# State-space layer: input products of every second state on TensorE, tiled state sums, twelve states read out by GpSimd

## Chip, cores and metric

The kernel runs on one core of a Trainium2 chip. The metric is the device time of one execution in microseconds (us); lower is better. A core has TensorE (PE, matrix products into PSUM), VectorE (DVE), ScalarE (ACT) and GpSimd (POOL), each with an in-order queue of its own, and SyncE (SP), which here only issues DMAs.

## What is computed

A language-model tower over 64 sequences of 128 tokens with 192 features: embedding and layer norm, attention, a layer of four experts, a bidirectional state-space layer, a layer of eight experts (two per token). The change touches the state-space layer alone. Of the reference, cut to what matters:

```python
def _mamba(x, W_in, conv_w, conv_b, W_xproj, W_dt, b_dt, A_log, D_param, W_out):
    xp, z = jnp.split(x @ W_in.T, 2, axis=-1)                  # 384 inner channels each
    xc = silu(causal_depthwise_conv(xp, conv_w, 4 taps) + conv_b)
    dt, Bt, Ct = jnp.split(xc @ W_xproj.T, [12, 12 + 16], axis=-1)
    dt = softplus(dt @ W_dt.T + b_dt)
    A = -jnp.exp(A_log)                                        # 384 x 16
    def step(h, inp):                                          # scan over the 128 tokens
        dt_t, B_t, C_t, x_t = inp
        dA = jnp.exp(dt_t[..., None] * A)
        h = dA * h + (dt_t * x_t)[..., None] * B_t[:, None, :]
        y = jnp.einsum('bdn,bn->bd', h, C_t)
        return (h, y)
    ...
    y = (y + xc * D_param) * silu(z)
    return y @ W_out.T
return 0.5 * (_mamba(x) + _mamba(x reversed in time) reversed)
```

## The kernel before, in words

The phases follow each other; the state-space phase (`mamba_phase`) takes the 64 sequences in 16 groups of four (512 tokens in the free dimension) and each group in two directions. The 384 channels are DC = 3 blocks (c) of 128 partitions, the NS = 16 states (n) are done one by one, so a half (one group, one direction) has 48 units p = 3n + c. In each unit

- ScalarE (`act_decay`) writes dA = exp(dt * A) for one block into one of four PSUM banks (`RING`, banks 3 to 6); where the bank held something else, it also zeroes the edge column of each sequence.
- GpSimd (`pool_dBx`, line 1804) writes the input products u * B_n of all three blocks at once into one of eight SBUF slots `xh`. B_n, the same for every partition, has been loaded by DMA (`sp_B_in`) from DRAM, where `sp_BC_out` stored it, broadcast over partitions.
- VectorE (`dve_scan`, line 1773) runs the recurrence h = dA * h + product over 512 columns.
- The read-out h * C_n is done by VectorE block by block (`dve_read`, line 1784) or, for the states in `BY_POOL` (8 in one direction, 6 in the other), by GpSimd in one instruction of three blocks (`pool_read`, line 1793).
- TensorE (`pe_sum`, line 1731) adds the read-outs of all states into banks 0 to 2 by matmuls with the identity, one per block and state; `pe_D` adds xc * D in the same way with a diagonal. A sum lags its scan by LAG = 3 states.

Beside these units run the steps of the next half, placed by hand at units given by the table `POS`: row additions and layer norm, transposes (`pe_zT`), input projection (`pe_x`, `pe_gate`), convolution by diagonal matrices (`pe_conv`, line 1579), projection to dt, B, C, softplus in three identity matmuls (`pe_sp`, line 1666, over u, lw and r; r is completed by a DMA that accumulates, issued by GpSimd in `pool_add`), u = dt * xc (`dve_u`, line 1675). TensorE's results of these steps pass through the one bank NB = 7, and each is copied out before the next. At the end of a group `dve_y` gates the sums and `pe_out` (line 1743) projects them. Each engine's queue follows the order of `slot`: in the units of a half, its own work (`main`) and the steps placed there.

Matmuls are in fp32; each shows as two weight loads and two matmul records in the trace, a transpose as one. The attention phase, which the change leaves as it is, has matmuls on 16 rows at four 32-row offsets (line 552, one after another for r = 0 to 3, each r to a bank of its own) and matmuls with 32 output columns at four 32-partition offsets of one bank (line 575), 12 matmuls each.

Of the kernel before, what the change touches and what calls it, by code (L numbers as in the profile page):

```python
# [15 lines left out]
P = 128  # L16
# [1306 lines left out]
PB, PD, PJ = 64, 96, 44  # L1323

# [30 lines left out]
def mamba_phase(nc, A, H, bank, K, Y, BCd, W):  # L1355
# [5 lines left out]
    with Phase(nc) as ctx:  # L1361
# [3 lines left out]
        NQ, QN = 8, 2  # L1365
        UNITS = NS * DC
        POS = {
            "y": (6, 7, 9), "pe_D0": (14, 15, 17), "pe_D1": (6, 16, 25), "pe_out": (17, 18), "out": (14, 15),
            "act_rows": (11, 13), "rows": (12, 14), "stats": 14, "rstd": 18, "norm": 40,
# [3 lines left out]
            "act_pj": (15, 10), "act_xc": (14, 8), "act_e": (23, 23), "act_w1": (23, 26), "act_ln": (26, 29),  # L1373
            "pe_sp0": (26, 36, 40), "act_sp0": (30, 39, 41), "u0": (34, 38, 41), "pe_sp1": (32, 38, 42), "act_sp1": (34, 38, 40),
            "u1": (32, 37, 40),
        }
        NB = 7
        BY_POOL = (0, 3, 4, 5, 10, 12, 13, 14), (0, 6, 9, 10, 11, 14)
        RING = ((3, 4, 5, 6) * 2 + (3, 4, 5, 3, 4, 5, 3) + (6, 4, 5, 3) * 8 + (6,),
                (4, 5, 3, 6, 4, 3, 5, 6) + (3, 4, 5, 6) * 10)  # L1380
        ROWS_BANK, ROWS_FROM, ROWS_TO = 6, 7, 15

        def before_in_bank(d, p):

            b, back = RING[d][p], 0
            while True:
                p -= 1
                if p < 0:
                    p, d, back = UNITS - 1, 1 - d, back + 1
                if RING[d][p] == b:  # L1390
                    return back, d, p
# [10 lines left out]
        dg, dgD = sb("dg", [P, DC, TAPS, P]), sb("dgD", [P, DC, P])  # L1402
# [4 lines left out]
        z = sb("z", [P, G, C])  # L1407
# [6 lines left out]
        lw = sb("lw", [P, DC, TOK])  # L1414
        gz = sb("gz", [P, DC, TOK])
# [27 lines left out]
        with nc.Block() as block:  # L1443
            @block.vector
            def _(dve):
# [3 lines left out]
                for c in range(DC):  # L1449
                    for k in range(TAPS):  # L1450
                        dve.tensor_scalar(dg[:, c, k, :], K.ident[:, :], cw[:, c, k:k + 1], None, ALU.mult)
# [610 lines left out]
```

## Time and profile before

| | |
|---|---|
| median of 3 runs | 4727.18 us (4723.77 to 4732.5) |
| profiled execution, first to last instruction | 4718.1 us |
| median less that span | 9.1 us |
| state-space phase in it | some 1145 to 3822 us |
| busy in the whole span: PE, DVE, ACT, POOL | 4271.6, 3251.1, 2430.7, 3212.3 us |

The profiled execution is one execution of the program; busy times, durations and waits below are its own. A group of instructions stands with its line, engine, operation, what it writes <- reads, its shape and its count. Matmuls are pipelined and their ends are modelled, so the distance from one start to the next tells more of TensorE's pace than the length of one.

### The profile page before, as it was taken

How to read it: one execution, taken by the hardware profiler on the slowest of the kernel's cores; microseconds unless marked ns; L12 is line 12 of the kernel's file. 1: busy time of each engine (PE TensorE's matmuls, PEld its weight loads, DVE VectorE, ACT ScalarE, POOL GpSimd, SP SyncE). 2: the span in 40 equal slices, each digit the busy share in tenths (PEclk: the TensorE clock that was granted, in tenths of full speed). 3: DMA queues.
4: the chain of work that ended last, by engine and by line, in shares of the span. 5: the costliest groups of instructions: out<-in, count | busy, mean ns of one | idle time of the engine just before them, and what ended most of it. 6: DMA issues, size and time to landing. Idle time of an engine off the chain costs nothing. (4 is left out here: it accounts for less than half of the span.)

```text
span 4718.1 us, 62490 instructions
## 1 busy us (share of the span) xinstructions
PE 4271.6 (91%) x16896; PEld 2235.4 (47%) x16896; DVE 3251.1 (69%) x5016; ACT 2430.7 (52%) x4880; POOL 3212.3 (68%) x1669
## 2 busy tenths in 40 slices
PE   7999986997899999999999999999999876999994
PEld 4666644664343443344334434433443334666673
DVE  5667773111699999999999999989999975111114
ACT  3555542122566666767676666667666633222221
POOL 3222222442799999999999999999999941444441
PEclk9999996998899999999999999999999987999997
DMA  1000011342334333334333333333333321333456
GB/s 35 21 20 20 20 53 59 108 127 76 107 114 125 115 118 116 121 109 121 122 112 115 112 121 118 116 118 113 117 107 123 114 67 45 110 116 112 127 169 219
DMA packets 267113, 478.79 MB, mean 101 GB/s; under 512 B 39404, under 2 KB 176444, under 8 KB 266908
## 3 DMA queue, kind: packets, MB, share of 16 engines
q1 hardware_dynamic: 235776, 403.02, 26.9%
q0 software_dynamic: 28032, 73.17, 6.1%
q14 instruction: 171, 1.40, 0.1%
q10 hardware_dynamic: 3100, 0.64, 0.1%
q8 instruction: 34, 0.56, 0.1%
HBM read 409.75 MB, written 41.81 MB: 96 GB/s over the span
## 5 line engine op out<-in xcount | busy, mean ns | idle before, releaser
L1804 POOL TENSOR_TENSOR m_xh<-m_u,m_Bb 128x1536 f32<-128x1536 f32 x512 | 1780.1, 3550 | 51.6 <-DVE m_u L1675 39.0
L1731 PE MATMUL bank<-m_xh,ident 128*128 128x512 f32 x3072 | 1455.1, 609 | 34.3 <-POOL m_xh L1793 34.3
L1773 DVE TENSOR_TENSOR_SCAN bank<-bank,m_xh 128x512 f32<-128x512 f32 x864 | 1038.9, 1216 | 44.5 <-ACT bank L1760 42.2
L1760 ACT ACTIVATE bank<-m_dt,m_Ac 128x508 f32<-128x508 f32 x1536 | 1024.9, 683 | 38.4 <-DVE m_xh L1773 38.4
L1731 PEld LDWEIGHTS bank<-m_xh,ident 128*128 128x128 f32 x3072 | 576.2, 194 | 820.0 <-issue 730.7
L1773 DVE TENSOR_TENSOR_SCAN m_xh<-bank,m_xh 128x512 f32<-128x512 f32 x672 | 787.8, 1207 | 64.8 <-ACT bank L1760 59.3
L1793 POOL TENSOR_TENSOR m_xh<-m_xh,m_Cb 128x1536 f32<-128x1536 f32 x224 | 794.0, 3544 | 4.3 <-DVE m_xh L1773 4.0
L1784 DVE TENSOR_TENSOR m_xh<-bank,m_Cb 128x512 f32<-128x512 f32 x864 | 581.3, 673 | 10.9 <-DMA m_Cb<-BC_rows 10.8
L1204 ACT ACTIVATE f1t_h<-bank,f1t_b 128x512 f32<-128x512 f32 (+1 forms) x276 | 147.6, 586 | 509.9 <-PE bank L1234 509.9
L1134 POOL DMA_INDIRECT rows_y<-f1t_y,f1t_home x142 | 139.9, 985 | 316.4 <-DVE f1t_y L1175 287.1
L1579 PE MATMUL bank<-m_xp,m_dg 128*128 128x512 f32 x768 | 351.9, 601 | 3.7 <-DVE m_u L1675 1.4
L1243 PE MATMUL bank<-f1t_w,f1t_h 128*128 128x192 f32 x1704 | 289.0, 329 | 19.4 <-ACT f1t_h L1204 19.4
L1243 PEld LDWEIGHTS bank<-f1t_w,f1t_h 128*128 128x128 f32 x1704 | 275.7, 190 | 31.6 <-issue 28.1
L1759 ACT COPY bank<-m_none 128x4 f32<-128x4 f32 x896 | 144.2, 161 | 260.5 <-DVE m_xh L1784 171.3
L1164 DVE COPY f1t_xTa<-bank 128x512 f32<-128x512 f32 (+1 forms) x46 | 26.2, 570 | 342.2 <-PE bank L1215 342.2
L97 POOL TENSOR_SCALAR ln_e_ve<-ln_e_mv 128x4 f32<-128x4 f32 x16 | 3.7, 229 | 348.2 <-DVE ln_e_mv L91 348.2
L1579 PEld LDWEIGHTS bank<-m_xp,m_dg 128*128 128x128 f32 x768 | 142.9, 190 | 201.6 <-issue 157.0
L373 DVE TENSOR_REDUCE mx<-bank 128x3 f32<-128x384 f32 x256 | 141.0, 551 | 113.4 <-PE bank L552 112.1
L1231 PE MATMUL bank<-f1t_xTa,f1t_w1a 128*128 128x512 f32 (+1 forms) x552 | 217.1, 516 | 1.6 <-DVE f1t_xTb L1167 1.6
L1175 DVE TENSOR_TENSOR f1t_y<-bank,f1t_b 128x192 f32<-128x192 f32 x142 | 50.8, 358 | 216.7 <-PE bank L1243 216.7
L1204 ACT ACTIVATE f0t_h<-bank,f0t_b 128x512 f32<-128x512 f32 (+1 forms) x132 | 71.9, 596 | 246.5 <-PE bank L1234 246.5
L454 ACT COPY ST<-bank 128x384 f32<-128x384 f32 x256 | 120.8, 472 | 143.0 <-PE bank L562 143.0
(367 smaller groups left out, 6148.3 us busy)
## 6 DMA issues: line engine op xcount, KB each, us to landing
m_Bb<-BC_rows SPq DMA_DIRECT2D x256, 512.0 KB, 4.8
m_Cb<-BC_rows SPq DMA_DIRECT2D x256, 512.0 KB, 4.0
f1t_w<-f_w SPq DMA_DIRECT2D x46, 576.0 KB
m_r<-m_dt POOLq DMA_DIRECT2D x32, 768.0 KB, 7.4
f1t_w1a<-f_w SPq DMA_DIRECT2D x46, 384.0 KB
f0t_w<-f_w SPq DMA_DIRECT2D x22, 576.0 KB
f1c_yg<-rows_y SPq DMA_DIRECT2D x16, 768.0 KB, 8.3
f1t_w1b<-f_w SPq DMA_DIRECT2D x92, 96.0 KB
```

What stands on the lines that cost most here:

```text
L373: dve.reduce_max(mx[:, u % NE, :], s_ps, AX).then_inc(s_mx, 1)
L1204: act.activation(h[b][:, m, 0:w * P], bank[:, HB[(s2 + m) % 4], 0:w * P], ACT.Gelu, bias=b1[b][:, m:m + 1]).then_inc(s_gelu, 1)
L1231: pe.matmul(o[f], w1a[b][:, (m + f) * P:(m + f + 1) * P], xTa[b][:, 0:w * P], start=True, stop=False)
L1243: mm = pe.matmul(bank[:, YB[j % 2], 0:C], h[b][:, m, j * P:(j + 1) * P], w2[b][:, m, :], start=(m == 0), stop=(m == HK - 1))
L1579: mm = pe.matmul(bank[:, front(c), :], dg[:, c, k, :], xp[:, c, :, o:o + P], start=(k == 0), stop=(k == TAPS - 1))
L1731: mm = pe.matmul(bank[:, c, :], K.ident[:, :], xh[n % NX][:, c, :], start=False, stop=(d == 1 and n == NS - 1))
L1759: act.copy(o[:, :, edge:edge + 1], none[:, :].unsqueeze(2))
L1760: act.activation(o[:, :, lo:hi], seqs(dt[d][:, c, :])[:, :, lo:hi], ACT.Exp, scale=Ac[:, c, n:n + 1]).then_inc(s_dA, 1)
L1773: dve.tensor_tensor_scan(o, bank[:, RING[d][p], way], xh[n % NX][:, c, way], 0.0, ALU.mult, ALU.add).then_inc(s_h, 1)
L1784: dve.tensor_tensor(xh[n % NX][:, c, :], bank[:, RING[d][p], :], Cb[q % RC][:, n % QN, :], ALU.mult).then_inc(s_prv, 1)
L1793: pool.tensor_tensor(v, v, Cb[q % RC][:, n % QN, :].unsqueeze(1).to_broadcast([P, DC, TOK]), ALU.mult).then_inc(s_prp, 1)
L1804: pool.tensor_tensor(xh[n % NX][:, :, :], u[d][:, :, :], Bb[q % RB][:, n % QN, :].unsqueeze(1).to_broadcast([P, DC, TOK]), ALU.mult).then_ ...
```

## The change

- `BY_PE`: for the eight odd states the input products come from TensorE. u is transposed per sequence (`pe_uT`, copied to `uT` by `act_uT`), B of these states too (`pe_BT`, `act_BT`). ScalarE writes, per state and sequence, B on the diagonal of a 128x128 matrix (`act_Bd`), and `pe_fill` multiplies: uT (stationary) by that diagonal, four matmuls of 128 columns per unit, into a PSUM ring bank, EARLY = 3 units ahead of the scan. The decay of these states goes to SBUF (`dA`, three buffers).
- GpSimd makes the products of the eight even states, and reads out twelve states in both directions (all but 2, 6, 10, 14).
- `pe_sum` and `pe_D` do the three blocks of a state in one step of 12 matmuls on 32x32 tiles (`turned`): block c's rows of strip q go to output strip (q + c) mod 4, so that the 12 tiles lie on different places of the array; weights for z and the output are permuted on the way in. `pe_conv` becomes four diagonal 32x32 tiles per tap.
- Rows are added to H by one accumulating DMA per group, issued by GpSimd (`pool_rows`), instead of load, two copies and two additions.
- B is loaded one state at a time into two buffers (before: two states, four buffers). The ring is plain p mod 4. Positions in `POS` change.

```diff
+QUADS, QP = 4, 32
+BY_PE = (1, 3, 5, 7, 9, 11, 13, 15)
+BY_GP = tuple(n for n in range(16) if n not in BY_PE)
...
-        BY_POOL = (0, 3, 4, 5, 10, 12, 13, 14), (0, 6, 9, 10, 11, 14)
+        BY_POOL = tuple(n for n in range(NS) if n not in (2, 6, 10, 14)), tuple(n for n in range(NS) if n not in (2, 6, 10, 14))
+        RINGS = 4
+        ring = lambda p: 3 + p % RINGS
...
-        RB, RC = 4, 2
+        RB, RC = 2, 2
...
-        NX, AHEAD, LAG = 8, 2, 3
+        NX, AHEAD, LAG, EARLY = 8, 2, 3, 3
+        NDA, NBD = 3, 2
...
+            def pool_rows(pool):
+                rows = Y[0:B * P, :].rearrange("(t p) c -> p t c", p=P)
+                pool.dma_start(H[:, bass.ds(gl * G, G), :], rows[:, bass.ds(gl * G, G), :], accum_op=ALU.add).then_inc(s_added, 16)
...
                 for k in range(TAPS):
                     o = k if d == 0 else 2 * (TAPS - 1) - k
-                    mm = pe.matmul(bank[:, front(c), :], dg[:, c, k, :], xp[:, c, :, o:o + P], start=(k == 0), stop=(k == TAPS - 1))
+                    for q in range(QUADS):
+                        i = slice(q * QP, (q + 1) * QP)
+                        mm = pe.matmul(bank[i, front(c), :], dg[i, c, k, :], xp[i, c, :, o:o + P], start=(k == 0), stop=(k == TAPS - 1))
...
+            def pe_uT(pe, c):
+                pe.wait_ge(s_u, s * DC + c + 1)
+                stand_alone(pe, K.go)
+                for b in range(G):
+                    mm = pe.transpose(bank[:, front(c), b * P:(b + 1) * P], u[d][:, c, b * P:(b + 1) * P], K.ident[:, :])
+                mm.then_inc(s_uTps, 1)
...
+        def turned(c):
+            for q in range(QUADS):
+                o = (q + c) % QUADS
+                yield slice(q * QP, (q + 1) * QP), slice(o * QP, (o + 1) * QP)
...
-        def pe_sum(pe, g, d, n, c):
+        def pe_sum(pe, g, d, n):
             if n not in BY_POOL[d]:
-                pe.wait_ge(s_prv, dve_reads(g, d, n) + c + 1)
-            elif c == 0:
+                pe.wait_ge(s_prv, dve_reads(g, d, n) + DC)
+            else:
                 pe.wait_ge(s_prp, pool_reads(g, d, n + 1))
-            mm = pe.matmul(bank[:, c, :], K.ident[:, :], xh[n % NX][:, c, :], start=False, stop=(d == 1 and n == NS - 1))
+            stand_alone(pe, K.go)
+            for c in range(DC):
+                for i, o in turned(c):
+                    mm = pe.matmul(bank[o, c, :], K.ident[i, i], xh[n % NX][i, c, :], start=False, stop=(d == 1 and n == NS - 1))
             mm.then_inc(s_red, 1)
...
+        def pe_fill(pe, g, d, p):
+            n, c = divmod(p, DC)
+            s = g * 2 + d
+            k = by_pe(n)
+            if c == 0:
+                pe.wait_ge(s_Bd, (s * NPE + k + 1) * G)
+            if k == 0:
+                pe.wait_ge(s_uT, s * DC + c + 1)
+            bank_free(pe, g, d, p)
+            stand_alone(pe, K.go)
+            for b in range(G):
+                t = slice(b * P, (b + 1) * P)
+                mm = pe.matmul(bank[:, ring(p), t], uT[d][:, c, t], Bd[k % NBD][:, b, :], start=True, stop=True)
+            mm.then_inc(s_fill, 1)
+
+        def act_Bd(act, g, d, n, b):
...
+            act.activation(Bd[k % NBD][:, b, :], K.ident[:, :], ACT.Identity, bias=none[:, 0:1], scale=BT[d][:, b, k:k + 1]).then_inc(s_Bd, 1)
...
+            if n in BY_PE:
+                dve.wait_ge(s_fill, fills(g, d, fill_no(p) + 1))
+                decay, add = dA[fill_no(p) % NDA][:, way], bank[:, ring(p), way]
+                if c == 0:
+                    slot_free(dve, g, d, n)
             else:
-                o = bank[:, RING[d][p], way]
-            dve.tensor_tensor_scan(o, bank[:, RING[d][p], way], xh[n % NX][:, c, way], 0.0, ALU.mult, ALU.add).then_inc(s_h, 1)
+                if c == 0:
+                    dve.wait_ge(s_dBx, s * NGP + by_gp(n) + 1)
+                decay, add = bank[:, ring(p), way], xh[n % NX][:, c, way]
+            o = xh[n % NX][:, c, way] if n in BY_POOL[d] else bank[:, ring(p), way]
+            dve.tensor_tensor_scan(o, decay, add, 0.0, ALU.mult, ALU.add).then_inc(s_h, 1)
```

## Rows read from the trace of the kernel before

**Rows 1.** The page: span, busy time, and two engines over 40 slices (tenths).

```profile
span 4718.1 us, 62490 instructions
PE 4271.6 (91%) x16896; PEld 2235.4 (47%) x16896; DVE 3251.1 (69%) x5016; ACT 2430.7 (52%) x4880; POOL 3212.3 (68%) x1669
...
PE   7999986997899999999999999999999876999994
...
DVE  5667773111699999999999999989999975111114
...
POOL 3222222442799999999999999999999941444441
```

**Rows 2.** Line 1828, the store of B and C, once a half.

```profile
L1828 SPq DMA_DIRECT2D BC_rows<-m_low x32: 348/360/427, 1182.6 to 3701.2; - x32
```

**Rows 3.** Windows: one whole group; length, busy (records) by engine, clock, DMA.

```profile
core 0: us, PE busy (x) PEld busy (x) DVE busy (x) ACT busy (x) POOL busy (x), PEclk, DMA share, GB/s
...
2393.00:2555.50 162.50, 156.44 (x367) 65.12 (x367) 148.56 (x171) 108.04 (x208) 159.34 (x53) 0.99 0.38 115
```

**Rows 4.** Timeline of GpSimd; start, length.

```profile
2326.17 3.65 POOL L1793 TENSOR_TENSOR m_xh<-m_xh,m_Cb 128x1536 f32<-128x1536 f32 x1
2329.56 3.65 POOL L1804 TENSOR_TENSOR m_xh<-m_u,m_Bb 128x1536 f32<-128x1536 f32 x1
2332.96 3.63 POOL L1793 TENSOR_TENSOR m_xh<-m_xh,m_Cb 128x1536 f32<-128x1536 f32 x1
```

**Rows 5.** Groups by line and shape, same group; busy, mean ns | idle before.

```profile
L1731 PE MATMUL bank<-m_xh,ident 128*128 128x512 f32 x192 | 90.0, 604 | 0.0
...
L1579 PE MATMUL bank<-m_xp,m_dg 128*128 128x512 f32 x48 | 21.9, 598 | 0.1
...
L1743 PE MATMUL bank<-m_wo,m_r 128*128 128x192 f32 x24 | 4.2, 326 | 0.0
```

**Rows 6.** Timeline of TensorE: state sums without a gap.

```profile
2304.62 7.89 PE L1731 MATMUL bank<-m_xh,ident 128*128 128x512 f32 x18
```

**Rows 7.** Timeline of VectorE.

```profile
2311.12 1.22 DVE L1773 TENSOR_TENSOR_SCAN bank<-bank,m_xh 128x512 f32<-128x512 f32 x1
2312.25 0.67 DVE L1784 TENSOR_TENSOR m_xh<-bank,m_Cb 128x512 f32<-128x512 f32 x1
2312.84 1.22 DVE L1773 TENSOR_TENSOR_SCAN bank<-bank,m_xh 128x512 f32<-128x512 f32 x1
```

**Rows 8.** Waits from 2080 to 3700 us, 20 halves; total, times, longest.

```profile
ACT m_dt L1671 <- PE bank L1666: 169.6, 60, 5.0
...
PE bank L1666 <- DMA m_r<-m_dt: 43.7, 20, 3.8
```

**Rows 9.** The page's DMA issues: times, size, us to landing.

```profile
m_r<-m_dt POOLq DMA_DIRECT2D x32, 768.0 KB, 7.4
```

**Rows 10.** Timeline of TensorE in the attention phase.

```profile
418.90 0.95 PE L552 MATMUL bank<-qT 16*128 16x128 f32 x24
419.78 1.13 PE L528 MATMUL bank<-zTa,wqp_a 128*128 128x512 f32 x2
...
421.60 0.49 PE L562 MATMUL bank<-ident,S 128*128 128x128 f32 x3
422.02 0.86 PE L575 MATMUL bank<-ST,V 128*32 128x128 f32 x24
422.82 0.70 PE L528 MATMUL bank<-zTa,wqp_a 128*128 128x512 f32 x1
```

**Rows 11.** Windows inside line 575: records in flight, PE then PEld.

```profile
422.00:422.04 0.04, 0.02 (x3) 0.02 (x3) 1.00 0.00 0
422.04:422.08 0.04, 0.04 (x4) 0.04 (x8) 1.00 0.00 0
422.28:422.32 0.04, 0.04 (x12) 0.04 (x6) 1.00 0.00 0
```

**Rows 12.** Timeline of ScalarE.

```profile
2389.63 0.15 ACT L1759 COPY bank<-m_none 128x4 f32<-128x4 f32 x1
2389.72 0.69 ACT L1760 ACTIVATE bank<-m_dt,m_Ac 128x508 f32<-128x508 f32 x1
2390.34 0.58 ACT L1568 COPY m_gz<-bank 128x512 f32<-128x512 f32 x1
2390.82 0.17 ACT L1759 COPY bank<-m_none 128x4 f32<-128x4 f32 x1
...
1441.64 1.85 ACT L1516 ACTIVATE m_z<-H,m_mrs,m_ln_rs 128x192 f32 x4
```

More of the change, by code:

```diff
@@ L1392, in mamba_phase @@
+        NPE, NGP = len(BY_PE), len(BY_GP)
+        by_pe = lambda n: sum(k < n for k in BY_PE)
+        by_gp = lambda n: sum(k < n for k in BY_GP)
+        fill_no = lambda p: by_pe(p // DC) * DC + p % DC
+        fills = lambda g, d, k: ((g * 2 + d) * NPE * DC) + k
         of_pool = lambda d, n: sum(k < n for k in BY_POOL[d])
@@ L1514, in act_norm @@
                 act.wait_ge(s_mrs, gl * 2 + 2)
+                if not first:
+                    stand_alone(act, K.go)
+                    act.wait_ge(s_spps, (s + 1) * DC)
                 for j in range(G):
@@ L1641, in act_ln @@
                 act.wait_ge(s_w1, s + 1)
-                if not first:
+                act.wait_ge(s_zTps, g * 2 + 2)
+                if d == 1:
+                    stand_alone(act, K.go)
                     act.wait_ge(s_spps, s * DC)
@@ L1675, in dve_u, with act_uT @@
                 dve.tensor_tensor(u[d][:, c, :], bank[:, front(c), :], xc[d][:, c, :], ALU.mult).then_inc(s_u, 1)
+            def pe_uT(pe, c):
[4 more added lines that the diff above has]
+                mm.then_inc(s_uTps, 1)
+            def act_uT(act, c):
+                act.wait_ge(s_uTps, s * DC + c + 1)
+                if c == 0 and deep:
+                    act.wait_ge(s_fill, (s - 1) * NPE * DC)
+                act.copy(uT[d][:, c, :], bank[:, front(c), :]).then_inc(s_uT, 1)
             todo = {"pe": [], "act": [], "dve": [], "pool": []}
@@ L1682, in chain @@
                 at = (lambda p: p - 100) if first else (lambda p: p)
-                for i in two:
-                    put("act", at(POS["act_rows"][i]), act_rows, i)
-                    put("dve", at(POS["rows"][i]), dve_rows, i)
+                put("pool", at(POS["rows"]), pool_rows)
                 put("dve", at(POS["stats"]), dve_stats)
@@ L1749, in act_decay @@
             lo, hi, edge = (1, P, 0) if d == 0 else (0, P - 1, P - 1)
-            o = seqs(bank[:, RING[d][p], :])
-            back, db, pb = before_in_bank(d, p)
             if p == 0:
                 act.wait_ge(s_sp, (g * 2 + d + 1) * DC)
-            if d == 0 and p == ROWS_TO and not (isinstance(g, int) and g == NG - 1):
-                act.wait_ge(s_added, g * 2 + 4)
-            elif back == 0 or later(g, d):
-                released(act, g if db <= d and back < 2 else g - 1, db, pb)
@@ L1758, in act_decay @@
-            if back or pb // DC not in BY_POOL[d] or d == 0 and p == ROWS_TO:
+            if n in BY_PE:
+                f = fill_no(p)
+                o = seqs(dA[f % NDA][:, :])
+                if f >= NDA:
+                    act.wait_ge(s_h, (g * 2 + d) * UNITS + BY_PE[by_pe(n) - 1] * DC + c + 1)
+                elif later(g, d):
+                    act.wait_ge(s_h, (g * 2 + d - 1) * UNITS + BY_PE[-1] * DC + c + 1)
+                zero = f < NDA
+            else:
+                o = seqs(bank[:, ring(p), :])
+                back, db, pb = before_in_bank(d, p)
+                bank_free(act, g, d, p)
+                zero = back or pb // DC in BY_PE or pb // DC not in BY_POOL[d]
@@ L1930, in main @@
                     n, c = divmod(p, DC)
-                    if c == 0 and not (end and n >= NS - AHEAD):
+                    if c == 0 and (n + AHEAD) % NS in BY_GP and not (end and n >= NS - AHEAD):
                         pool_dBx(pool, *at_step(g, d, n + AHEAD))
@@ L2028, in layout @@
     import numpy as np
+    turned = np.concatenate([c * P + (q - c) % QUADS * QP + np.arange(QP) for c in range(DC) for q in range(QUADS)])
+    as_is = np.arange(DC * P)
     g = lambda n: np.asarray(inputs[n])
```

259 lines of the change are left out of this document (146 added, 113 removed), and 3 rows, old and new, of the table POS.

## The prediction

> **What bounds the kernel now.** I read the page first: over the span TensorE is busy most, but in the slices of the state-space phase GpSimd stands at nine tenths or more in almost every one, and TensorE and VectorE too [rows 1]. So three engines run near their limit there, and the question is which has no slack. The unit for that is one half (one direction of one group of four sequences: 16 states of 3 blocks). The store of B and C happens once a half; 32 of them from 1182.6 to 3701.2 us give 2518.6/31 = 81.2 us a half [rows 2]. Only what shortens that counts, 32 times.
>
> The windows of one whole group (two halves, 162.5 us) show GpSimd 159.3 busy, TensorE 156.4, VectorE 148.6, ScalarE 108.0 [rows 3]. Busy time of overlapping instructions misleads, so I take start-to-start distances where an engine runs without a gap.
> - GpSimd: a product or read-out of 128x1536 starts every 3.40 us [rows 4]. Before, a half has 16 products and 7 read-outs: 23 x 3.40 = 78.2 of 81.2. The other 3.0 are the start of the accumulating DMA, the norm's small operations and waits.
> - TensorE: each fp32 matmul leaves two records. The group has 368 expected and 367 shown [rows 3]: 192 for state sums, 48 for the convolution, 24 of 192 columns for the output [rows 5], 8 transposes, and 96 more of 512 columns by the code. 18 records of 512 columns take 7.89 us with an end of 0.6: 0.43 each [rows 6]. 336 x 0.43 + 24 x 0.17 + 8 x 0.11 = 149.5, so 74.7 a half, 92%.
> - VectorE: a scan costs 1.13 us and a read-out 0.59 [rows 7]: 48 x 1.13 + 27 x 0.59 (on average of the two directions) + some 4.5 for u, y, rows, output and statistics = 74.6.
> - ScalarE: 54 [rows 3].
>
> So GpSimd sets the pace with some 1 us of true idle time a half, and TensorE and VectorE follow 6 us behind. The chain of waits shows what else holds the in-order queues: ScalarE waits for TensorE's softplus sum (169.6 us in 20 halves), and TensorE for the DMA into m_r (43.7 in 20, 2.2 a half) [rows 8].
>
> **The change, engine by engine, a half.**
>
> GpSimd: 8 products instead of 16, 12 read-outs instead of 7: 20 x 3.40 = 68.0; of the 3.0 beside them some 1.6 stay of known work, and the rows' accumulating DMA adds 0.4. That is 70.0, or 71.2 with the same idle time.
>
> VectorE: 15 read-outs fewer, -8.8, and the two additions of rows go: about 65.5. Scans keep one PSUM and one SBUF operand; only which is which changes, so 1.13 stays.
>
> ScalarE: two row copies go, three copies of u's transpose come at 0.5 (a copy of 512 columns, start to start) [rows 12], and 32 activations of 128x128 that write B on a diagonal. Not in the trace; a copy of 4 columns takes 0.09 start to start and 192 columns with a scale column 0.44 [rows 12]. I take 0.30, between them: 9.6, bounds 3 and 14. ScalarE comes to 65, bounds 58 and 69. Fewer zeroed edges take some 1 off. That is hidden as long as TensorE or GpSimd needs more; with the 8.5 a half that it waits for L1666 today (169.6 / 20 [rows 8]) it would reach 73.5, so it has lost most of its cover.
>
> TensorE, where I expect the bound:
> - State sums. 48 matmuls of 128x128 (41.3 us) become 16 steps of 12 matmuls on 32x32 tiles, and D's three (2.6) one such step. If the tiles run at once a step costs two passes, 0.86. The attention stage shows half of that: 12 matmuls on four row strips (L552) and 12 on four column strips (L575) take 24 records of 128 columns in 0.95 and 0.86 us to the last end, 0.80 to 0.88 until the next step starts [rows 10]; one after another they would take 24 x 0.11 = 2.6. The windows inside L575 show three records started in 40 ns, four in flight, later twelve by the modelled ends [rows 11]. So four streams at once are seen over row strips and over column strips; twelve over both are not. Lower bound 0.86, upper bound 3 x 0.86 = 2.58 if the three blocks of a state follow each other. It is nearest to L575, whose streams share all rows as the three blocks here do, so I take 0.86 and 0.08 for staggered starts: 17 x 0.94 = 16.0.
> - Switches between full and tiled passes: L552 and L575 cost 0.88 and 0.80 against 6 waves of 0.11 = 0.66 [rows 10], so about 0.2 a step. 16 sums and 3 convolution blocks: 19 x 0.2 = 3.8.
> - Products of every second state: 24 units of 4 matmuls, 8 records of 128 columns. Bounds: a quarter of the 512-column record, 0.107, and the 192-column record, 0.17. Transposes of 128 columns with a weight load each start 0.11 to 0.12 apart (three of L562, 0.49 with an end of 0.27) [rows 10]; I take 0.115: 22.1, bounds 20.5 and 33.
> - 12 transposes of u, 12 x 0.11 = 1.3; the four small ones of B, 0.9.
> - Convolution: each 128x128 matmul becomes four diagonal tiles. At once, they cost the same 12 x 0.86 = 10.3; softplus 7.7, dt and projection 5.2, x or gate 5.2, output 2.0, row transposes 0.5 are unchanged.
> Sum: 16.0 + 3.8 + 22.1 + 2.2 + 30.9 = 75.0. TensorE then has more work than GpSimd's 70.0, so it takes over as the bound, at about its old load.
>
> TensorE's queue is in order, and a product unit is issued only three units before its scan (some 4 us). Its waits used to be covered by sums that lag three states. Now behind a TensorE wait (softplus for the DMA into m_r, 7.4 us from issue to landing [rows 9]) stand products that VectorE needs next. I add what TensorE waits now for that DMA, 2.2, rounded to 2.0: 77.0 a half. The loads of B shrink by half or more and keep one state of lead; the C loads keep two buffers, each freed by GpSimd's later read-outs, with some 3 units to spare; I cost both at nothing.
>
> Sum: (77.0 - 81.2) x 32 = -134. Once: transposing B and u before the first half +3. The profiled execution: 4718.1 - 131 = 4587; the median of the runs is 9.1 above that span, so 4596, and I say 4595.
>
> **A rule against it.** The attention stage's row strips (L552) write four different banks, its column strips (L575) one; four row strips into one bank, as the convolution and each block's sum do here, no row shows. "TensorEngine Tiling (Array Packing)", Gotcha 1, in the Trainium skill says that different row tiles cannot access the same PSUM bank simultaneously. Taken word for word this would serialise them (the fourth rival). I weigh it low, since each strip writes its own 32 partitions, as L575's do.
>
> **Rivals.**
> 1. GpSimd stays the bound (TensorE at its lower ends: products 20.5, switches near 0, sums 13.8, some 68). 71.2 a half, so -320 + 3: 4410. For: 0.107 is what the columns cost. Against: switch gaps are visible.
> 2. Coupling. Nothing overruns, but TensorE, in the loop of VectorE's scans, loses 2.5 to 7 us more a half in round trips over its one front bank (now also for u's transposes): 79.5 to 84, 4675 to 4820. For: ScalarE's long waits for L1666. Decides from 4.2 us a half.
> 3. The three blocks of a state pass one after another, sharing row strips: a step costs 2.66, +1.72 x 17 = +29 a half: 106, about 5520. This is the slower case by one mechanism; it decides as soon as a step costs above 1.2 us. For: in L552 the three column blocks of one strip do follow each other. Against: L575. Half of it (each block's second pass ahead of the next block, 1.72 a step) gives 5020. "TensorE: Matmul & The Clock Gate", part 3, in the Trainium skill says weight loads overlap running matmuls only where the row group differs, which would bring this rival about; it also reports sixteen tiles at once, which would not.
> 4. Row strips of one bank exclude each other: sums and D 17 x 9.4 more, convolution 31 more: some 270 a half, above 10,000 us.
>
> **How the numbers follow.** Forecast (74 to 79 a half, 4500 to 4660) 0.45; rival 1, 0.15; rival 2, 0.20; rival 3, 0.12, its half 0.05; rival 4, 0.02; 0.01 left. The range must leave out no more than 0.2: from 4420 (most of rival 1) to 4860 (all of rival 2). A measurement of this kernel can tell about 0.2%, 9 us, which is 0.3 us a half. Faster: 0.45 + 0.15 + 0.04 of rival 2 = 0.64. Same 0.04, the narrow part of rival 2 about 81.2 a half. Slower: the rest, 0.32.
>
> **What would show it.** Start to start, a state's sum of 24 records should take about 0.95 us and be followed within 0.2 by the next step; 8 records of a product unit 0.92; halves 77 apart by the store of B and C; in the windows TensorE without idle time, GpSimd at 90%, VectorE at 85, ScalarE at 85. Wrong would be: a sum over 1.2 us, GpSimd without gaps, or VectorE waiting for TensorE's products while TensorE stands at L1666 or u's transposes.

## The result and the profile after

The changed kernel takes 5416.3 us (5413.1 to 5416.7, four runs), the kernel before in the same comparison 4729.8 (4723.8 to 4733.7): ratio 1.1456, 95% interval 1.1438 to 1.1473. It is slower by 686 us; the forecast was 4595, range 4420 to 4860. The prediction was wrong, in sign too.

The page of the changed kernel, span, busy time and two engines over 40 slices, answers to [rows 1]:

```profile
span 5414.6 us, 102448 instructions
PE 4577.8 (85%) x35776; PEld 2682.9 (50%) x35776; DVE 2970.8 (55%) x4508; ACT 2853.3 (53%) x5840; POOL 2920.9 (54%) x1589
...
PE   7999879968888888888888888888888887799994
DVE  5777641116665666666566656666666676411114
...
POOL 2222124417676676667666766766766674244442
PEclk9999979979898898888888989888998988899997
```

GpSimd and VectorE, at nine tenths before, stand mostly at six or seven, and TensorE at eight. No engine is full, and yet the phase is longer. The store of B and C (now line 1917) gives the length of a half, as [rows 2] did:

```profile
L1917 SPq DMA_DIRECT2D BC_rows<-m_low x32: 318/326/430, 1184.9 to 4381.1; - x32
```

(4381.1 - 1184.9)/31 = 103.1 us a half, against 81.2. All of the loss is there: 21.9 x 32 = 701 us, against 697 between the two profiled executions.

Windows of the same stretch as [rows 3], and one of 400 us, by the same columns:

```profile
core 0: us, PE busy (x) PEld busy (x) DVE busy (x) ACT busy (x) POOL busy (x), PEclk, DMA share, GB/s
2400.00:2800.00 400.00, 340.10 (x2984) 179.18 (x2982) 255.17 (x270) 257.93 (x514) 269.77 (x90) 0.89 0.26 73
...
2393.00:2555.50 162.50, 135.76 (x1180) 73.62 (x1179) 107.77 (x117) 106.43 (x210) 111.18 (x39) 0.88 0.27 73
```

Times 103.1/400, a half holds 69.5 us of GpSimd's work, 66.5 of ScalarE's, 65.8 of VectorE's: the forecast had 70, 65 and 65.5. These three sums were right to 2 us, and each engine now stands idle for a third of the half. TensorE is 87.7 busy against 75 forecast, at a granted clock of 0.89 (0.99 in [rows 3]). Busy time counts more than starts do: before, the window had 78.2 a half where the prediction's sum gave 74.7. That leaves some 9 us that the forecast did not have.

Single operations cost what was forecast, too. TensorE's timeline (start, length; in brackets the idle time before and who ended it), where it runs without a gap:

```profile
2586.23 1.11 PE L1776 MATMUL bank<-m_xc,m_dgD 32*32 32x512 f32 x24
2587.27 1.16 PE L1815 MATMUL bank<-m_Bd,m_uT 128*128 128x128 f32 x8
2588.36 1.11 PE L1787 MATMUL bank<-m_xh,ident 32*32 32x512 f32 x24
...
2593.70 1.11 PE L1787 MATMUL bank<-m_xh,ident 32*32 32x512 f32 x24
2594.75 1.16 PE L1815 MATMUL bank<-m_Bd,m_uT 128*128 128x128 f32 x8
```

D's step of 24 records takes 1.04 us to the next start and a state's sum 1.05, product units 1.09 (forecast: 0.94 and 0.92, and 0.2 for each switch between full and tiled). The twelve tiles run at once: 24 records of 0.43 one after another would take 10.3. GpSimd's operations start 3.40 apart as before (2570.17 to 2573.57, shown below).

What fills the half are waits. The list of waits, 2080 to 3900 us, 17.7 halves (total, times, longest), against [rows 8]:

```profile
POOL m_xh L1888 <- DVE m_xh L1868: 321.2, 125, 7.1
...
DVE m_xh L1868 <- ACT m_dA L1847: 177.1, 61, 7.7
ACT m_xc L1602 <- PE bank L1594: 171.4, 51, 10.2
...
POOL m_xh L1899 <- PE bank L1787: 152.6, 33, 7.6
ACT m_dt L1654 <- PE bank L1644: 152.3, 45, 6.7
DVE m_xh L1868 <- PE bank L1815: 150.4, 47, 6.2
DVE m_xh L1868 <- ACT bank L1847: 124.5, 47, 4.8
```

Read it as a circle. GpSimd's read-outs (L1888) wait for scans, scans (L1868) for ScalarE's decays (L1847) and for products (L1815), ScalarE at the convolution (L1602) and at dt (L1654) for TensorE, and GpSimd's products (L1899) for TensorE's sums. Most waits are short (the first line is 2.6 each), and each engine is late because of another. One place shows how; first TensorE:

```profile
2570.60 3.62 PE L1594 MATMUL bank<-m_xp,m_dg 32*32 32x512 f32 x32
2575.27 3.65 PE L1594 MATMUL bank<-m_xp,m_dg 32*32 32x512 f32 x32 [1.04 <-ACT m_xc L1602]
2579.81 3.22 PE L1594 MATMUL bank<-m_xp,m_dg 32*32 32x512 f32 x28 [0.89 <-ACT m_xc L1602]
2582.44 0.80 PE L1787 MATMUL bank<-m_xh,ident 32*32 32x512 f32 x8
...
2584.25 2.05 PE L1815 MATMUL bank<-m_Bd,m_uT 128*128 128x128 f32 x16
```

then ScalarE,

```profile
2574.44 0.69 ACT L1602 ACTIVATE m_xc<-bank,m_cb 128x512 f32<-128x512 f32 x1 [3.83 <-PE bank L1594]
...
2578.98 0.69 ACT L1602 ACTIVATE m_xc<-bank,m_cb 128x512 f32<-128x512 f32 x1 [1.68 <-PE bank L1594]
```

VectorE,

```profile
2575.83 1.23 DVE L1868 TENSOR_TENSOR_SCAN bank<-bank,m_xh 128x512 f32<-128x512 f32 x1 [3.33 <-ACT bank L1847]
...
2585.53 1.22 DVE L1868 TENSOR_TENSOR_SCAN m_xh<-m_dA,bank 128x512 f32<-128x512 f32 x1 [6.17 <-PE bank L1815]
```

and GpSimd:

```profile
2570.17 3.44 POOL L1899 TENSOR_TENSOR m_xh<-m_u,m_Bb 128x1536 f32<-128x1536 f32 x1 [1.31 <-DMA m_Bb<-BC_rows]
2573.57 3.43 POOL L1888 TENSOR_TENSOR m_xh<-m_xh,m_Cb 128x1536 f32<-128x1536 f32 x1
2584.55 3.46 POOL L1899 TENSOR_TENSOR m_xh<-m_u,m_Bb 128x1536 f32<-128x1536 f32 x1 [7.55 <-PE bank L1787]
```

The next half's convolution stands at positions 3, 4 and 5 of TensorE's in-order queue. Its three blocks share one front bank, so each waits for ScalarE's copy of the one before: they start 4.6 us apart, 3.6 of them their own matmuls and 1.0 and 0.9 the wait. ScalarE meanwhile stands 3.83 us at that copy with the present half's decays behind it, and VectorE stands 3.33. Then the product, which is behind the third block, keeps VectorE 6.17, and the state's sum, also behind it, keeps GpSimd 7.55. GpSimd's idle time before was 1.6 us a half in [rows 3].

The clock adds to it. Windows of the changed kernel in a stage of dt and gate, and TensorE's timeline there:

```profile
2505.00:2512.00 7.00, 5.64 (x37) 2.26 (x36) 4.10 (x5) 3.49 (x8) 5.92 (x2) 0.76 0.36 123
2512.00:2520.00 8.00, 8.00 (x32) 1.93 (x32) 3.35 (x3) 4.65 (x9) 1.54 (x2) 0.57 0.50 125
2520.00:2527.00 7.00, 6.42 (x53) 3.55 (x52) 2.54 (x3) 6.54 (x9) 6.70 (x2) 1.00 0.43 84
```

```profile
2515.09 1.98 PE L1787 MATMUL bank<-m_xh,ident 32*32 32x512 f32 x24
2517.00 2.08 PE L1573 MATMUL bank<-m_zTa,m_win_a 128*128 128x512 f32 x2
...
2522.21 1.02 PE L1573 MATMUL bank<-m_zTa,m_win_a 128*128 128x512 f32 x2
```

The levels are 0.50 (1.2 GHz) and 1.00 (2.4 GHz); windows of 1 us show 0.50 from 2506 to 2509 and from 2513 to 2519. At the lower level a sum takes 1.9 us and two records 2.0; from 2520 on, at 2.4 GHz, two records take 0.95. Before the first fall, from 2499 to 2505, TensorE had been busy for 4.7 of 6 us; between the two stretches it stood idle for 1.36 in one piece. Such stretches hold part of its 87.7 busy microseconds.

### The profile page after: what moved, and what is told of

Same layout as the page of the kernel before. It is cut to its first block and busy times, and to the rows that moved or that the text cites. A ratio compares the mean times of both kernels' runs of the same rounds, so it can differ in the third digit from the quotient of the medians.

```text
span 5414.6 us, 102448 instructions
## 1 busy us (share of the span) xinstructions
PE 4577.8 (85%) x35776; PEld 2682.9 (50%) x35776; DVE 2970.8 (55%) x4508; ACT 2853.3 (53%) x5840; POOL 2920.9 (54%) x1589
## 5 line engine op out<-in xcount | busy, mean ns | idle before, releaser
L1888 POOL TENSOR_TENSOR m_xh<-m_xh,m_Cb 128x1536 f32<-128x1536 f32 x384 | 1327.7, 3462 | 579.4 <-DVE m_xh L1868 579.4
L1868 DVE TENSOR_TENSOR_SCAN m_xh<-m_dA,bank 128x512 f32<-128x512 f32 x768 | 908.4, 1207 | 572.7 <-ACT m_dA L1847 325.7
L1815 PE MATMUL bank<-m_Bd,m_uT 128*128 128x128 f32 x6144 | 953.5, 311 | 216.9 <-DVE m_xh L1879 127.7
L1815 PEld LDWEIGHTS bank<-m_Bd,m_uT 128*128 128x128 f32 x6144 | 859.0, 219 | 552.1 <-issue 550.7
L1899 POOL TENSOR_TENSOR m_xh<-m_u,m_Bb 128x1536 f32<-128x1536 f32 x256 | 882.9, 3449 | 337.3 <-PE bank L1787 256.2
L1787 PE MATMUL bank<-m_xh,ident 32*32 32x512 f32 x12288 | 663.8, 669 | 1.9 <-POOL m_xh L1888 1.9
L1868 DVE TENSOR_TENSOR_SCAN m_xh<-bank,m_xh 128x512 f32<-128x512 f32 x384 | 446.6, 1205 | 232.8 <-ACT bank L1847 216.5
L1847 ACT ACTIVATE m_dA<-m_dt,m_Ac 128x508 f32<-128x508 f32 x768 | 545.5, 711 | 0.6
L1847 ACT ACTIVATE bank<-m_dt,m_Ac 128x508 f32<-128x508 f32 x768 | 525.5, 684 | 0.0
L1825 ACT ACTIVATE m_Bd<-ident,m_none,m_BT 128x128 f32<-128x128 f32 x1024 | 493.0, 482 | 53.6 <-PE bank L1815 53.1
L1868 DVE TENSOR_TENSOR_SCAN bank<-bank,m_xh 128x512 f32<-128x512 f32 x384 | 458.4, 1213 | 108.6 <-ACT bank L1847 108.6
L1602 ACT ACTIVATE m_xc<-bank,m_cb 128x512 f32<-128x512 f32 x96 | 66.0, 687 | 315.2 <-PE bank L1594 315.2
```

Of the source, the lines that this page charges most:

```text
L1787: mm = pe.matmul(bank[o, c, :], K.ident[i, i], xh[n % NX][i, c, :], start=False, stop=(d == 1 and n == NS - 1))
L1815: mm = pe.matmul(bank[:, ring(p), t], uT[d][:, c, t], Bd[k % NBD][:, b, :], start=True, stop=True)
L1825: act.activation(Bd[k % NBD][:, b, :], K.ident[:, :], ACT.Identity, bias=none[:, 0:1], scale=BT[d][:, b, k:k + 1]).then_inc(s_Bd, 1)
L1847: act.activation(o[:, :, lo:hi], seqs(dt[d][:, c, :])[:, :, lo:hi], ACT.Exp, scale=Ac[:, c, n:n + 1]).then_inc(s_dA, 1)
L1868: dve.tensor_tensor_scan(o, decay, add, 0.0, ALU.mult, ALU.add).then_inc(s_h, 1)
L1888: pool.tensor_tensor(v, v, Cb[q % RC][:, n % QN, :].unsqueeze(1).to_broadcast([P, DC, TOK]), ALU.mult).then_inc(s_prp, 1)
```

## The experiments

Eighteen kernels, each profiled once beside a run of the kernel before (4722.9 to 4730.9 us), and the one with the tiled sums alone timed four times. "A half" below is the difference of two times over 32, where nothing else is said from the changed kernel's 5416.3. The code shows the heart of each edit, shortened at the dots. All runs of the kernel before lie within 0.3%, 0.5 us a half. Where the computation is altered, the edit says so.

**Parts of the change taken back.** Theories, by the names that the expectations use: *work* (TensorE's work was underestimated), *ScalarE* (its work of 65 with 32 diagonals sets the half), *lockstep* (a product three units ahead of its scan, a scan behind its product), *chain* (the steps that prepare the next half, one after another over one bank).

First, the products as plain transposes of u, without the product with B, some 11 us a half less on TensorE:

```
-  mm = pe.matmul(bank[:, ring(p), t], uT[d][:, c, t], Bd[k % NBD][:, b, :], ...)
+  mm = pe.transpose(bank[:, ring(p), t], uT[d][:, c, t], K.ident[:, :])
```

> The product matmuls are replaced by plain transposes back, one record of 128 columns each instead of two: TensorE has some 11 us less work a half (24 units x 0.46), the rest waits for the same things. It leaves out the multiplication by B for the odd states. The changed kernel takes 103.1 us a half. Lockstep theory (products stand in TensorE's in-order queue between steps of the next half, three units ahead of a scan, and TensorE can't run ahead of VectorE any more): 98 to 103 a half, 5250 to 5415 us. Work theory (TensorE's own work with the products fills the time): 92 a half, about 5060 us.

Measured: 5255.1 us, clock 0.889: 5.0 a half less, at the low edge of the lockstep range. Half of the work taken out comes back as time, so it was not the whole of the bound.

Second, one diagonal a state instead of four (B of the first sequence is used for all), 9.4 us a half less on ScalarE:

```
-  pe.wait_ge(s_Bd, (s * NPE + k + 1) * G)
+  pe.wait_ge(s_Bd, s * NPE + k + 1)
-  for b in range(G):      # diagonals made
+  for b in range(1):
```

> One diagonal of B per state instead of four (the products of the other three sequences use that of the first, so three quarters of them are not the layer's): ScalarE has 24 x 0.39 = 9.4 us less work a half. ScalarE theory (the diagonals overload ScalarE, whose decays come late): 93.7 a half, about 5115 us. Lockstep theory: ScalarE mostly waits in its queue for TensorE, so 98 to 102, 5250 to 5380 us. Work theory of TensorE: unchanged, 5415.

Measured: 5357.1, 1.9 a half less. ScalarE's sum of work is not the bound.

Third, only the positions: ScalarE's steps four to five units behind TensorE's instead of two to three, stages spread over more of the half:

```
-  "act_conv0": (6, 8, 10), ... "pe_conv0": (3, 4, 5), "pe_pj": (11, 11), ...
+  "act_conv0": (10, 13, 16), ... "pe_conv0": (5, 8, 11), "pe_pj": (17, 13), ...
```

> The same work on every engine; only the units at which steps of the next half stand in the queues change: ScalarE's steps stand four to five units behind TensorE's step that they wait for (before two to three), TensorE's steps three units apart, the norm four units later. Lockstep theory: 85 to 93 a half, 4830 to 5090 us. Work theory and ScalarE theory: unchanged, 5350 to 5450 us.

Measured: 5249.0, 5.2 a half less with nothing taken out of any engine: the lockstep theory had 4830 to 5090, the other two no gain, and no range holds. Products now stop VectorE longer (324.6 us in 1820, before 150.4), and GpSimd stands 145.1 us at the start of the accumulating DMA, which these positions put too early.

**Down the ladder.** The next three kernels take more and more out of the changed one. First, the scans add u in place of the product, decays all in PSUM; diagonals and u's transposes are still made (output without B in half of the states):

```
-  if n in BY_PE: ... pe_fill(pe, g, d, p + EARLY)
+  pass
-  decay, add = dA[...][:, way], bank[:, ring(p), way]
+  decay, add = bank[:, ring(p), way], u[d][:, c, way]
```

> No products by TensorE: the scans of odd states add u as it is (the multiplication by B is left out for them), their decay stands in the PSUM ring as before the change; transposes of u and the B diagonals are still made, but nobody waits for them. VectorE no longer waits for TensorE. Lockstep theory: back to GpSimd's pace, 72 to 80 a half, 4420 to 4680 us. Work theory: 103 less 24 = 79, about 4650. ScalarE theory: ScalarE keeps its diagonals, so 95 or more, above 5150 us.

Measured: 5077.3, 10.6 a half less. By lockstep it should have been near 4420 to 4680, by ScalarE's work above 5150; neither holds. With every product gone GpSimd is at 75%, TensorE at 73%, ScalarE at 73% and the clock at 0.82 in 2400 to 2800 us.

The same without any diagonal:

```
-  for b in range(G):      # diagonals
+  for b in range(0):
```

> The kernel without TensorE products (92.6 us a half) and now without the 32 diagonals of B on ScalarE as well (12 us less of its work a half). ScalarE theory: 82 a half or less, about 4740 us. Chain theory (the next half's steps, convolution to u's transpose, form one chain through the one front bank, which has become longer and stands tighter in the queues): 88 to 92 a half, 4930 to 5060 us.

Measured: 4913.2, 5.1 a half less again for 12 us of ScalarE's work. Both expectations missed, the chain's by 17 us.

And without the steps on B's rows and u's transposes, the others nearly all at the old kernel's positions:

```
-  put("pe", POS["pe_BT"][d], pe_BT);  put(.. pe_uT ..);  put(.. act_uT ..)
```

> As the one before, and also without the steps that transpose B and u, with the remaining steps of the next half at the units where they stood before the change (the row steps, the norm, sums and output as in the changed kernel). What is left of the change is GpSimd's 20 operations, tiled sums and convolution and the accumulating DMA. Chain theory: 72 to 82 a half, 4420 to 4740 us. If the tiled steps themselves or the DMA were the cause, it stays at 88 or more, above 4930.

Measured: 4781.3, 4.1 less, clock 0.858, between the two expectations (up to 4740, above 4930). As steps and positions changed together, their shares are not told apart. This kernel ("the shortened kernel" below) has less work than the kernel before on each of the four engines and is still 1.8 a half slower than that in the run beside it (4722.9). Windows, 2400 to 2800 us, of it, and of the kernel before over the same stretch:

```profile
2400.00:2800.00 400.00, 308.82 (x2648) 104.44 (x2631) 316.89 (x339) 251.43 (x427) 338.99 (x115) 0.81 0.30 88
```

```profile
2400.00:2800.00 400.00, 385.71 (x900) 158.73 (x899) 366.78 (x416) 271.50 (x518) 392.40 (x127) 0.99 0.37 115
```

The changed kernel with one convolution tap of four, 7.7 us a half less on TensorE, all of it in the chain:

```
-  for k in range(TAPS):
+  for k in (TAPS - 1,):
```

> The changed kernel with one of the convolution's four taps (three are left out): TensorE has 9 x 0.86 = 7.7 us less work a half, and all of it in the chain that ScalarE waits for, unlike the 11 us of half the product work, which gave 5.0 a half. Chain theory: 8 to 12 a half less than 103.1, 5030 to 5160 us. If only the amount of TensorE work counts, 7.7 of it give 3.5 a half, 5300 us.

Measured: 5211.1, 6.4 a half less, again between the two (up to 5160, near 5300). Microseconds taken from a chain step come back at 0.83 each, those from products (the first run) at 0.45, those from diagonals at 0.20 to 0.43; each is one run.

Four states by TensorE instead of eight, with nine states read out by GpSimd instead of twelve:

```
-  BY_PE = (1, 3, 5, 7, 9, 11, 13, 15)
+  BY_PE = (1, 5, 9, 13)
```

> Products of four states (1, 5, 9, 13) by TensorE instead of eight, nine states read out by GpSimd: TensorE 11.8 us less, ScalarE 6 us less, GpSimd 21 operations (71.4), VectorE 21 block read-outs (71). The output is the layer's. Chain theory: the chain keeps its length, so it gives half of what the kernel without products gave, 96 to 99 a half, 5180 to 5290 us. Work theory: 103.1 - 11.8 = 91, 5030 us. Still slower than before under both.

Measured: 5261.6, 4.8 a half less, as the chain theory had it. But GpSimd waits 432 us in 1820 for rows of B, which come one state at a time.

**The clock.** Every kernel so far had a lower clock than the kernel before. If the emptied TensorE loses its clock and with it the time, more work should help. Zero weights added into the sum banks change no result:

```
+  for c in (0, 1):
+      for i, o in turned(c):
+          mm = pe.matmul(bank[o, c, :], zw[:, 0:QP], xh[n % NX][:, c, :], start=False, ...)
```

> The kernel without products, diagonals, B and u transposes (4781 us, granted clock 0.858), with TensorE given more to do: after the twelve tiled records of each state sum, eight records of 128 rows by 32 columns whose weights are all zero are added into two of the three sum banks, so the sums are unchanged. About 1.7 us of work more per state at full clock, 28 us a half on an engine that was busy 77 of 100. Clock theory (the emptied TensorE is granted a lower clock, and the steps of the next half, whose 512-column records then lie 1.0 us apart and not 0.43, set the half): the clock of the span is 0.93 or more and the time falls although work was added, 4690 to 4770 us. Queue theory (the length of TensorE's in-order queue sets the chain, the clock is a by-product): 4850 to 5300 us, slower than 4781.

> The changed kernel (5416 us, clock 0.901), with four records of 128 rows by 32 columns and zero weights added into one sum bank after each state sum: about 0.9 us a state, 14 us a half, to an engine that by the forecast had 75 of work in a half and by the trace was 81 to 90 of 100 busy. Clock theory: the clock rises to 0.94 or more and the time falls, 5200 to 5400 us. Queue theory: the half grows by most of the 14 us, 5550 to 5870 us.

> The kernel without products, diagonals, B and u transposes (4781 us, clock 0.858), with the state sums and D as full 128 by 128 matmuls of 512 columns again (three a state, some 2.6 us, in place of twelve tiled ones of 1.0; the layout of the banks stays turned, so D and the sums land in other rows than the gate expects). TensorE's work rises by some 26 us a half. Clock theory: the clock returns to 0.94 or more, the time falls below 4781, to 4650 to 4750 us. Queue theory: not below 4781, 4800 to 5000 us. GpSimd has 20 operations of 3.4 us a half, 68 us, so 4400 us would be its bound.

Measured: 5146.9, 5584.0 and 5032.5 us, each at a clock of 0.934: 11.4 a half more for 28 us of ballast, 5.2 more for 14, 7.9 more for 26 of full sums. (The second has the ballast in one bank only.) The clock rose about as expected, and the time rose with it, as the queue theory had it (the third by more than its range, up to 5000). So the clock theory, as the cause of the whole, falls. As the ballast brings clock and work together, the clock's own share stays open. On a TensorE that in the shortened kernel was idle for 23 of 100, 30 to 41% of the added work came out as time.

Then the tiled sums and D alone, on the kernel before:

```
-  mm = pe.matmul(bank[:, c, :], K.ident[:, :], xh[n % NX][:, c, :], ...)   # per block
+  for c in range(DC):
+      for i, o in turned(c):
+          mm = pe.matmul(bank[o, c, :], K.ident[i, i], xh[n % NX][i, c, :], ...)
```

> The kernel before with one part of the change alone: D and the state sums as twelve tiled 32 by 32 matmuls each, with the turned weights and one count a state; convolution, products, readout and positions as before apart from y (8, 9, 10) and D (13 and 7). TensorE's work falls by some 26 us a half, GpSimd keeps its 23 operations of 3.4 us, 78 of the 81.2 us of a half. Work theory: GpSimd sets the half as before, within 0.5% of the kernel before, 4710 to 4755 us. Clock theory: the emptied TensorE is granted a lower clock (0.85 to 0.92 against 0.957) and the steps of the next half come later: 4760 to 4950 us.

Measured: 4764.0 against 4730.4, ratio 1.0071 (1.0055 to 1.0088), clock 0.877. TensorE has 26 us a half less to do, and it is 1.1 a half slower. GpSimd sets the half, as before: in 2400 to 2800 us it is 384.63 busy of 400. The time lies at the low edge of the clock theory's range and 9 us above the other's, and the clock is as the former had it: here the lower clock and all else in the edit cost one microsecond net, hidden behind GpSimd.

**The chain by itself.** The state loop is done for one of the four sequences: decays, products, scans, read-outs and sums take 128 of 512 columns. Every wait is kept and every instruction but three of the four matmuls of a product. First the changed kernel, then the one before, then the shortened one.

```
-  o[:, :, lo:hi] ...  slice(None) ...  xh[n % NX][:, :, :] ...  xh[n % NX][i, c, :]
+  o[:, 0:1, lo:hi] ...  slice(0, P) ...  xh[n % NX][:, :, 0:P] ...  xh[n % NX][i, c, 0:P]
```

> The changed kernel with the state loop done for one of the four sequences: decays, products, scans, readouts, GpSimd's products and the state sums take 128 of the 512 columns, all else (every instruction, wait and DMA, the diagonals, and all steps that prepare the next half) is as it was. Output of the other three sequences lacks its states. What lies outside the 32 halves is 5416.3 less 32 times 103.1, 2117 us. Chain theory (the steps of the next half are by themselves about as long as the half): 90 to 103 us a half, 5000 to 5416 us. Mixing theory (the chain alone is short, and it is the sharing of the in-order queues with the loop that stretches both): 50 to 70 us a half, 3720 to 4360 us.

> The kernel before with the state loop done for one of the four sequences in the same way. The chain has no step on B's rows, no u transposes and no diagonals here. Chain theory: shorter than in the changed kernel by the added round trips (three for u, one for B, some 15 to 20 us a half) but not by more. Mixing theory: 40 to 60 us a half, 3400 to 4050 us, and within 15 us of the changed kernel's. GpSimd's 23 operations of a quarter of the columns are at least 20 us a half.

> The kernel without products, diagonals, B and u transposes with the state loop done for one of the four sequences. If what the changed kernel's chain has more than the one before's are the B and u steps and the diagonals, this one lies within 4 us a half of the quarter run of the kernel before; if the tiled steps and their stops (convolution, D, sums) lengthen it, it is 5 us or more above that.

Measured: 4702.9, 4249.9 and 4411.3 us. Store of B and C and windows, changed kernel:

```profile
L1917 SPq DMA_DIRECT2D BC_rows<-m_low x32: 317/327/572, 1184.0 to 3709.2; - x32
```

```profile
2000.00:3400.00 1400.00, 1088.50 (x10763) 490.73 (x10762) 420.04 (x1193) 890.68 (x2268) 379.66 (x404) 0.82 0.32 92
```

and the kernel before:

```profile
L1828 SPq DMA_DIRECT2D BC_rows<-m_low x32: 347/426/1252, 1184.5 to 3283.5; - x32
```

```profile
2000.00:3400.00 1400.00, 1168.30 (x3903) 611.59 (x3902) 592.49 (x1924) 790.59 (x2115) 509.14 (x554) 0.88 0.44 140
```

The shortened kernel:

```profile
L1908 SPq DMA_DIRECT2D BC_rows<-m_low x32: 317/326/430, 1183.7 to 3429.7; - x32
```

```profile
2000.00:3400.00 1400.00, 1033.81 (x10756) 398.31 (x10755) 452.37 (x1326) 717.29 (x1715) 419.41 (x446) 0.78 0.35 101
```

(3709.2 - 1184.0)/31 = 81.5 us a half are left of 103.1, and (3283.5 - 1184.5)/31 = 67.7 of 81.2; the shortened one has (3429.7 - 1183.7)/31 = 72.5 of 83.0. Neither expectation for the changed kernel holds (it was 90 to 103, or 50 to 70). The kernel before came out 13.8 below the changed one, where the chain theory had 15 to 20 and the mixing theory 15 at most, but with a half of 40 to 60. The shortened one lies 4.8 above it, between the 4 and the 5 of its two cases. With GpSimd and VectorE 27 and 30% busy, ScalarE 64 and TensorE 78, the changed kernel still needs 81.5 a half, the length of the whole half before. (The loop's small operations are still in the queues, so the bare chain is somewhat shorter in all three.) By this measure, of the 21.9 us lost, 13.8 are a longer chain, 8.1 a worse mixing with the loop (21.6 over the chain, 13.5 before). Of the 13.8, 9.0 go with products, diagonals, B's and u's steps and the positions that changed for them, and 4.8 remain in the shortened kernel (tiled steps and their stops, the ring of banks, the few new positions, the clock; not told apart).

The clock is in these lengths too. An estimate from the rows: a mean clock of 0.89 between levels 0.5 and 1 means 22 to 23 of 103.1 us at the lower one, in which TensorE gets 11 us of full-clock work done and loses 11; in the kernel before (0.99 of 81.2) it loses 0.8. So at most some 10 of the 21.9 us are the clock's own, if TensorE was busy all through those stretches and all of it stood in the chain. In the quarter runs the same sum gives 14.7 (0.82 of 81.5), 8.1 (0.88 of 67.7) and 16.0 (0.78 of 72.5): up to 6.6 of the 13.8, and all of the 4.8 could be clock.

**Repairs.** Products two units ahead instead of three:

```
-  NX, AHEAD, LAG, EARLY = 8, 2, 3, 3
+  NX, AHEAD, LAG, EARLY = 8, 2, 3, 2
```

> The changed kernel with the products made two units ahead of their scan instead of three, so that TensorE waits at a product for a scan that is one unit older. Lockstep theory (TensorE stops in its queue at the products and holds the chain behind it): 3 us a half or more faster, below 5320 us. If the scans then wait for the products instead, or if the products' waits are no cause: 5370 to 5600 us.

Measured: 5315.7, 3.1 a half less, just what lockstep asked for: the stops at products are a part of the cause.

All three repairs together:

> The changed kernel with three edits together that computes the same: products two units ahead (alone 100 us less), four states by TensorE instead of eight, with nine read out by GpSimd (alone 155 less), and the positions of ScalarE's steps four to five units behind TensorE's (alone 167 less), now with the accumulating DMA's start moved three to six units later. If the three act on separate waits their gains add: some 4990 us. If they act on one chain, whose own length the quarter run shows as 81 us a half: 5050 to 5200 us. Either way above the kernel before.

Measured: 5387.8, clock 0.860. Above both expectations (4990, and 5050 to 5200): the gains of 3.1, 4.8 and 5.2 shrank to 0.9. The list of waits shows what came in their place:

```profile
POOL m_xh L1899 <- DMA m_Bb<-BC_rows: 416.2, 100, 9.0
...
ACT m_dt L1700 <- PE bank L1695: 247.0, 54, 14.3
...
PE bank L1695 <- DMA m_r<-m_dt: 175.1, 18, 15.6
```

GpSimd waits for rows of B, and the accumulating DMA, started later, now stops TensorE for up to 15.6 us at the softplus sum with the products behind it.

The last one leaves out the four states and puts the DMA back one unit behind the exponential:

> The changed kernel with two of the three edits, and without the one that put more states on the slowly fetched rows of B: products two units ahead, and ScalarE's steps four to five units behind TensorE's with GpSimd's accumulating DMA one unit after the exponential as in the changed kernel. Four states by TensorE is left out, because the three together made GpSimd wait 416 us for rows of B in 1820. If the two act on separate waits, 5416 less 100 less 167: some 5150 us. If they act on the same waits (TensorE's queue held at a product, ScalarE's at a step that TensorE has not done): 5200 to 5280 us. If the positions were made for three units ahead and the later products meet them badly: over 5300 us.

Measured: 5268.4, 4.6 a half less, no more than the positions gave alone, and in the range for repairs that act on the same waits.

No version that computes the layer beat the kernel before.

## Why the prediction was wrong

- **What bounds the kernel before**: right. GpSimd at 78 of 81; with TensorE lightened by 26 us a half (tiled sums alone) nothing was gained. What it missed: the chain under it is already some 67.7 us long (the quarter run), so a half of 77 left a longer chain 9 us in all.
- **GpSimd 70.0, VectorE 65.5, ScalarE 65**: right, 69.5, 65.8, 66.5. A diagonal costs 0.39 from start to start (2566.93 to 2567.32 on ScalarE), not 0.30, inside its bounds: 12.5 a half in place of 9.6.
- **Tiled sums 16.0, switches 3.8, products 22.1**: nearly right. 17 x 1.05 = 17.9 with the switch inside, against 19.2 (16.0 and 16 switches of 0.2); products 24 x 1.0 to 1.09 = 24 to 26. Rivals 3 and 4 are out: twelve tiles into three banks, four row strips to each, take 1.05 us, where three blocks in turn would take 2.66 and 24 records one after another 10.3; and a block of the convolution, four row strips into one bank, takes 3.62 for 32 records, against 3.44 for its columns. The rule weighed against it, "TensorEngine Tiling (Array Packing)", Gotcha 1, in the Trainium skill, by which different row tiles cannot access one PSUM bank at the same time, does not show here; the strips write partitions of their own. Nor does the one of "TensorE: Matmul & The Clock Gate", part 3, in the Trainium skill, by which weight loads overlap running matmuls only where the row group differs: the three blocks share their row strips and do not follow one another.
- **The failed step**: "TensorE then has more work than GpSimd's 70.0, so it takes over as the bound", and its 77.0 as 75.0 of work and 2.0 for one wait. The half was taken as the longest engine's work and one wait. No engine's work sets it: the longest, TensorE, is 87.7 busy of 103.1 and the others 70 or less. In its place stands a chain of steps over all engines, which was never added up: by the quarter runs it had 67.7 us in the kernel before, got round trips for u and B, and came to 81.5 with three quarters of the loop's columns gone. The 2.0 for waits measured 28, the 103.1 less 75.0: 15.4 are TensorE idle, some 9 more busy time, which the lower clock can account for (11 by the estimate above), and 3.5 the way of counting.
- **Loads of B, put at nothing**: GpSimd waited 35.1 us for them in 17.7 halves, 2.0 a half; small against the rest.
- **Rival 2, coupling** named the right mechanism, priced at 2.5 to 7 us. Its sign, VectorE waiting for products, is there (150.4 us in 17.7 halves), in the place shown behind the convolution and not behind the softplus sum. It took the price from waits as they were in a kernel where TensorE's sums lag three states and so cover its stops. Products three units ahead have no such cover, and where ScalarE's step stands two or three units behind TensorE's, a late step stops both queues: products nearer to their scan gave 3.1 a half back, steps farther apart 5.2. That these are the two reasons for the wrong price is argued from this, not shown.
- **The clock** was left at its old level. It fell from 0.957 to 0.901 over the span. It is not the whole cause (with ballast it rose and the time did too), its share in the stretches at 1.2 GHz is real (sums 1.9 us), and how much of the 22 us that is, up to the estimate of some 10, stays open.
- **Rival 1** (4410) needed GpSimd as the bound, and GpSimd has gaps everywhere.

## What to carry to other kernels

Before work is moved between engines in a pipeline that is nine tenths full on three of them, add up the dependent chain of one period as well as each engine's work: shrinking the loop to a quarter of its columns, with all waits kept, bounds it from above in one run. In in-order queues a step that waits costs what stands behind it; so here a step shortened in the chain gave back 0.8 of its time and work outside it 0.2 to 0.45, and repairs of one chain did not add up. Twelve 32x32 tiles at once are cheap (1.05 us against 2.6), but freeing an engine that was not the bound gained nothing, and its granted clock came out lower.

## What the runs showed of the hardware

- 24 records of twelve 32x32 fp32 tiles, spread over four row and four column strips and three banks, take 1.05 us until the next step; three full 512-column matmuls took 2.6.
- The granted clock of the span was lower in kernels in which TensorE had less to do in a half: 0.957 before, 0.877 with tiled sums alone, 0.858 in the shortened kernel, and 0.934 in that with zero-weight ballast or full sums.
- A record of 512 columns starts 0.43 us after the last in the kernel before and some 1.0 after it at the lower level, and a tiled sum takes 1.9 in place of 1.05.
